# Second attention: two 64-row halves of the array instead of the whole array

## The reference

```python
q, k, v = split(x @ Wqkv + bqkv)          # q: 256 wide, k and v: 64 wide each
q = q.reshape(b, s, 16, 16)               # 16 heads of 16
k = tile(k.reshape(b, s, 4, 16), 4)       # 4 key heads, head h uses key head h % 4
v = tile(v.reshape(b, s, 4, 16), 4)
prob = softmax(q k^T / 16)                # not causal: all 1024 keys
x = layernorm(x + (prob v) @ Wout + bout)
```

## Time and profile before

| | us |
|---|---|
| device time, median of 3 runs | 2425.41 |
| lowest and highest | 2424.32, 2425.58 |
| profiled execution, first to last instruction (its span) | 2423.6 |
| PE busy | 2238.1 (92%) |
| DVE busy | 1561.5 (64%) |
| ACT busy | 1196.9 (49%) |
| DVE's reduction of 512 columns (L1068), mean of 512 | 0.683 |

### The profile page before, as it was taken

The page is one execution under the profiler, slowest core; times in us unless marked ns, Lnnn a source line. Parts: engine busy times, 40 slices in busy tenths (PEclk is TensorE's granted clock), DMA queues, the critical chain, the costliest instruction groups (busy, mean ns, idle before and its releaser), DMA issues. The chain is left out here.

```text
span 2423.6 us, 36462 instructions
## 1 busy us (share of the span) xinstructions
PE 2238.1 (92%) x11264; PEld 1719.0 (71%) x11264; DVE 1561.5 (64%) x2879; ACT 1196.9 (49%) x2397; POOL 567.5 (23%) x550
## 2 busy tenths in 40 slices
PE   6999999999999999679999669999998689999996
PEld 5888888888888888558788434554543458877885
DVE  4666666666666666646566558887882436655665
ACT  4555555555555555344334316666666334433442
POOL 2333333333333333112222210000000012222221
PEclk9999999999999999879999869999999769999998
DMA  2000000000000000011111061212210011111111
GB/s 66 16 17 16 15 16 16 16 15 15 15 15 15 15 9 1 1 38 46 46 46 46 9 145 24 30 27 37 31 26 12 1 38 46 48 50 39 46 49 47
DMA packets 45297, 73.19 MB, mean 30 GB/s; under 512 B 6651, under 2 KB 21798, under 8 KB 44710
## 3 DMA queue, kind: packets, MB, share of 16 engines
q1 hardware_dynamic: 44710, 72.10, 12.2%
q10 hardware_dynamic: 512, 0.13, 0.0%
HBM read 64.74 MB, written 7.34 MB: 30 GB/s over the span
## 5 line engine op out<-in xcount | busy, mean ns | idle before, releaser
L1399 POOL TENSOR_TENSOR a_pr<-a_pr,a_rinv 128x128 f32<-128x128 f32 (+7 forms) x256 | 294.0, 1149 | 598.0 <-DVE a_rinv L1636 598.0
L1068 DVE TENSOR_REDUCE a1m_part<-psum 128x1 f32<-128x512 f32 x512 | 320.8, 683 | 93.4 <-PE psum L914 92.8
L1040 ACT ACTIVATE a1m_pt<-psum 128x512 f32<-128x512 f32 x512 | 265.6, 604 | 115.7 <-PE psum L934 107.6
L647 DVE SCALAR_TENSOR_TENSOR f_hid<-psum,f_bias_now,f_act_s 128x512 f32<-128x512 f32 x168 | 126.0, 750 | 267.0 <-ACT f_act_s L604 196.9
L504 POOL TENSOR_TENSOR f_lo_gu<-f_raw_gu,f_hi_gu 128x512 fp32r<-128x512 f32 x84 | 109.1, 1298 | 783.2 <-ACT f_hi_gu L579 783.2
L604 ACT ACTIVATE f_act_s<-psum,f_bias_now 128x512 f32<-128x512 f32 x168 | 115.7, 689 | 337.4 <-PE psum L71 263.8
L1563 ACT ACTIVATE a_pth<-psum 128x512 fp32r<-128x512 f32 (+3 forms) x384 | 174.6, 490 | 193.6 <-PE psum L1455 192.6
L69 PE MATMUL psum<-xh,f_hi_gu 128*128 128x512 f32 x672 | 265.9, 396 | 2.0 <-POOL f_lo_gu L504 1.3
L71 PE MATMUL psum<-xh,f_lo_gu 128*128 128x512 f32 x672 | 264.3, 393 | 0.0
L70 PE MATMUL psum<-xl,f_hi_gu 128*128 128x512 f32 x672 | 263.6, 392 | 0.0
L914 PE MATMUL psum<-a_ks,a_qm 128*128 128x512 f32 x512 | 224.2, 452 | 23.6 <-DMA a_qm<-a_qd 20.9
(11 more groups left out here) (225 smaller groups left out, 4937.4 us busy)
## 6 DMA issues: line engine op xcount, KB each, us to landing
f_raw_gu<-in_gu SPq DMA_DIRECT2D x84, 256.0 KB, 2.7
a_wr<-in_qkv SPq DMA_DIRECT2D x32, 384.0 KB, 3.1
f_raw_dn<-in_down SPq DMA_DIRECT2D x84, 128.0 KB, 2.0
a_qm<-a_qd SPq DMA_DIRECT2D x48, 128.0 KB, 5.3
a_qt<-a_qd SPq DMA_DIRECT2D x48, 128.0 KB, 3.9
yT<-in_xT SPq DMA_DIRECT2D x4, 512.0 KB, 6.1
a_wor<-in_o SPq DMA_DIRECT2D x16, 128.0 KB, 2.0
a_qd<-a1p_hi SPq DMA_DIRECT2D x2, 1024.0 KB, 14.0
```

The source lines that it names most:

```text
L1040: act.activation(pt[:, kp % 2, g, k, :], st_ps[:, bank(place(c, kp, g, k)), :], ACT.Exp, scale=1.0 / HD1).then_inc(exp_done, 1)
L1068: dve.tensor_reduce(part[:, c, q, g, half:half + 1], mx_ps[:, bank(at + g * 2 + half), :], AX.X, ALU.max).then_inc(mx_taken, 1)
L1399: pool.tensor_tensor(pr[:, j, 0:n], pr[:, j, 0:n], rinv[:, j:j + 1].to_broadcast([P, n]), ALU.mult).then_inc(p_done, 1)
```

## The change

Only `grouped_attention` is changed. Keys and queries lie twice in the height of the array: key heads 0 and 1 on rows 0 to 47, heads 2 and 3 on rows 64 to 111 (`HALFP`), two heads side by side in each half. The row of ones and of maxima is row 48 of each half, and every matmul of maxima or scores takes 48 or 49 rows of one half. The order pairs them: in a step `i` the maxima are those of a head of one half and the two scores those of the heads of the other half. One q tile (`qq`, three places) replaces `qm` and `qt`. Maxima go to a ring of two places of two banks each: both halves of the keys, one reduction over 1024 columns straight into `negm`. The turns of `zt` and `negm` take one place of that ring, at step 9 of a unit. `values` is called once for each key pair (16 records). SP, not ACT, sends the maxima. The loops are written out. The new main part (`...` marks what is left out):

```diff
     ROWS = 3 * HD1
-    MROW = 64
+    HALFP = 64
...
-    NS = NK * G1
-    NM = NQ * G1 * 2
-    NR = 3
-    ORDER = ("s0t1", "s0tv1")
+    QSLOT = 3
     W = KV1 // G1 * 2
     with Phase(nc, tag, psum) as ph:
         qd = [nc.dram_tensor(f"{tag}_qd{s}", (D + KV1, T), F32, kind="Internal").ap() for s in range(2)]
-        ks = ph.sb("ks", [P, B, G1, S], F32R)
+        ks = ph.sb("ks", [P, B, 2, S], F32R)
         vs = ph.sb("vs", [P, NTOK, G1, W])
-        qm = ph.sb("qm", [P, NCH, G1, CH], F32R)
-        qt = ph.sb("qt", [P, NCH, G1, CH], F32R)
+        qq = ph.sb("qq", [P, QSLOT, 2, CH], F32R)
...
-                    for r, src in enumerate((qd[0], qd[1], qd[0])):
-                        sp.dma_start(ks[r * HD1:(r + 1) * HD1, b, :, :].bitcast(F32),
-                                     src[D:D + KV1, b * S:(b + 1) * S].rearrange("(g p) t -> p g t", p=HD1)).then_inc(k_in, 16)
+                    for r in range(2):
+                        for x, src in enumerate((qd[0], qd[1], qd[0])):
+                            p0, d0 = r * HALFP + x * HD1, D + r * 2 * HD1
+                            sp.dma_start(ks[p0:p0 + HD1, b, :, :].bitcast(F32),
+                                         src[d0:d0 + 2 * HD1, b * S:(b + 1) * S].rearrange("(s p) t -> p s t", p=HD1)).then_inc(k_in, 16)
...
-                pool.memset(ks[:].bitcast(F32), 0.0).then_inc(cleared, 1)
-                pool.wait_ge(cleared, 1)
-                pool.memset(ks[MROW:MROW + 1, :, :, :].bitcast(F32), 1.0).then_inc(cleared, 1)
+                pool.memset(ks[:].bitcast(F32), 1.0).then_inc(cleared, 1)
+                pool.memset(vs[:], 0.0).then_inc(cleared, 1)
                 pool.wait_ge(cleared, 2)
-                pool.memset(vs[:], 0.0).then_inc(cleared, 1)
+                pool.memset(vs[:, :, :, HD1:HD1 + 1], 1.0).then_inc(cleared, 1)
                 pool.wait_ge(cleared, 3)
-                pool.memset(vs[:, :, :, HD1:HD1 + 1], 1.0).then_inc(cleared, 1)
-                for t in (qm, qt):
-                    pool.memset(t[:].bitcast(F32), 0.0).then_inc(cleared, 1)
-                pool.wait_ge(cleared, 6)
...
-            st_ps = am.ps([P, NR, CH])
-            mx_ps = am.ps([P, NR, CH])
+            mx_ps = am.ps([P, 2, 2, CH])
+            st_ps = am.ps([P, 3, CH])
...
-            misc_ps = am.ps([P, CH])
...
+            UNITS = [(b, j, c) for b in range(B) for j in range(QUADS) for c in range(NCH)]
+            LAST = len(UNITS) - 1
+            STEPS = NK * G1 // 2
+            GROUPS = (0, 2, 1, 3)
+            TURN = 9
+            def head_of(i):
+                return i // G1, GROUPS[i % G1]
+            def maxima_at(u, i):
+                v, n = (u + 1, STEPS // 2 + i) if i < STEPS // 2 else (u + 2, i - STEPS // 2)
+                return (v, n) if v <= LAST else None
+            FIRST = [(0, i) for i in range(STEPS)] + [(1, i) for i in range(STEPS // 2)]
+            class Ring:
+                def __init__(self):
+                    self.n, self.maxima, self.turns = 0, 0, 0
+                    self.freed = []
+                def place(self):
+                    self.n += 1
+                    return (self.n - 1) % 2, self.freed[self.n - 3] if self.n > 2 else None
+                def a_max(self):
+                    at = self.place()
+                    self.maxima += 1
+                    self.freed.append(((mx_taken, self.maxima),))
+                    return at
+                def a_turn(self, u, with_z, with_m):
+                    at = self.place()
+                    self.freed.append((((z_done, u),) if with_z else ()) + (((m_kept, u + 2),) if with_m else ()))
+                    return at
...
+                def fetch(u):
+                    b, j, c = UNITS[u]
+                    if u >= QSLOT:
+                        sp.wait_ge(st_ready, (u - QSLOT + 1) * 2 * STEPS)
+                    for r in range(2):
+                        for x, src in enumerate((qd[0], qd[0], qd[1])):
+                            d0 = (j * G1 + r * 2) * HD1
+                            rows = src[d0:d0 + 2 * HD1, b * S + c * CH:b * S + (c + 1) * CH]
+                            p0 = r * HALFP + x * HD1
+                            sp.dma_start(qq[p0:p0 + HD1, u % QSLOT, :, :].bitcast(F32),
+                                         rows.rearrange("(s p) t -> p s t", p=HD1)).then_inc(q_in[u % QSLOT], 16)
+                def send_maxima(u):
+                    sp.wait_ge(m_kept, u + 1)
+                    for g in range(G1):
+                        p0 = (g // 2) * HALFP + ROWS
+                        sp.dma_start(qq[p0:p0 + 1, u % QSLOT, g % 2, :].bitcast(F32),
+                                     mrow[g * NQ:(g + 1) * NQ, u % 2, :].bitcast(F32)).then_inc(m_in[u % QSLOT], 16)
+                for u in range(QSLOT):
+                    fetch(u)
+                for u in range(LAST + 1):
+                    send_maxima(u)
+                    if u >= 1 and u + QSLOT - 1 <= LAST:
+                        fetch(u + QSLOT - 1)
...
+                def room(at):
+                    for sem, n in at[1] or ():
+                        pe.wait_ge(sem, n)
+                    return at[0]
+                def maxima(u, i, half, bank):
+                    b, j, c = UNITS[u]
+                    q, g = head_of(i)
+                    p0 = (g // 2) * HALFP
+                    if i == 0 and half == 0:
+                        pe.wait_ge(q_in[u % QSLOT], (u // QSLOT + 1) * 96)
+                    m = pe.matmul(mx_ps[:, bank, half, :], qq[p0:p0 + ROWS, u % QSLOT, g % 2, q * P:(q + 1) * P],
+                                  ks[p0:p0 + ROWS, b, g % 2, half * CH:(half + 1) * CH], start=True, stop=True)
+                    if half == 1:
+                        m.then_inc(mx_ready, 1)
+                def scores(u, i, k):
+                    b, j, c = UNITS[u]
+                    n = u * 2 * STEPS + 2 * i + k
+                    kt, g = i // 2, (1 - i % 2) * 2 + k
+                    p0 = (g // 2) * HALFP
+                    if i == 0 and k == 0:
+                        pe.wait_ge(m_in[u % QSLOT], (u // QSLOT + 1) * 64)
+                    if n >= 3:
+                        pe.wait_ge(exp_done, n - 2)
+                    pe.matmul(st_ps[:, n % 3, :], ks[p0:p0 + ROWS + 1, b, g % 2, kt * P:(kt + 1) * P],
+                              qq[p0:p0 + ROWS + 1, u % QSLOT, g % 2, :], start=True, stop=True).then_inc(st_ready, 1)
+                def values(u, kp):
+                    b, j, c = UNITS[u]
+                    pe.wait_ge(exp_done, (u * NP + kp + 1) * 2 * G1)
+                    if kp == 0 and u >= 1:
+                        pe.wait_ge(zt_done, u)
+                    for k in range(2):
+                        kt = kp * 2 + k
+                        for g in range(G1):
+                            m = pe.matmul(acc_ps[g * W:(g + 1) * W, :], vs[:, b * NK + kt, g, :], pt[:, kp % 2, k, g, :],
+                                          start=kt == 0, stop=kt == NK - 1, tile_position=(0, g * W))
+                    m.then_inc(pv_done, 1)
+                def turn(u, with_z, with_m, bank):
+                    if with_z:
+                        pe.wait_ge(zt_done, u)
+                        for q in range(NQ):
+                            m = pe.transpose(mx_ps[:, bank, 0, q * P:(q + 1) * P], zt[:, q * P:(q + 1) * P], ident[:])
+                        m.then_inc(z_turned, 1)
+                    if with_m:
+                        pe.wait_ge(mx_taken, (u + 2) * STEPS)
+                        pe.transpose(mx_ps[0:G1 * NQ, bank, 1, 0:P], negm[:, (u + 1) % 2, :], ident[:]).then_inc(m_turned, 1)
+                for u, i in FIRST:
+                    bank = room(ring.a_max())
+                    for half in range(2):
+                        maxima(u, i, half, bank)
+                    if (u, i) == (0, STEPS - 1):
+                        turn(-1, False, True, room(ring.a_turn(-1, False, True)))
+                for u in range(LAST + 1):
+                    for i in range(STEPS):
+                        ahead = maxima_at(u, i)
+                        if ahead:
+                            bank = room(ring.a_max())
+                            if ahead:
+                                maxima(*ahead, k, bank)
+                            scores(u, i, k)
+                        if i % 4 == 1 and (u, i) != (0, 1):
+                            values(*((u, i // 4 - 1) if i > 1 else (u - 1, NP - 1)))
+                        if i == TURN and (u > 0 or u < LAST):
+                            turn(u, u > 0, u < LAST, room(ring.a_turn(u, u > 0, u < LAST)))
+                values(LAST, NP - 1)
+                turn(LAST + 1, True, False, room(ring.a_turn(LAST + 1, True, False)))
...
+                def keep_maxima(u):
                     act.wait_ge(m_turned, u + 1)
+                    if u >= 2:
+                        act.wait_ge(m_in[(u - 2) % QSLOT], ((u - 2) // QSLOT + 1) * 64)
```

(102 more changed lines are left out.)

172 lines of the change are left out of this document (21 added, 151 removed).

## The result

The changed kernel takes 2463.31 us (median of 4 runs, 2456.22 to 2467.13) against 2425.49 (4 runs, 2424.32 to 2427.80). The ratio is 1.0152, with a 95% interval of [1.0133, 1.0172]: 1.5% slower, clear of noise. The forecast was 2402.5, with a range of 2386 to 2446.

The account below looks back on a forecast made before the run. PE, busy 92%, was taken to set the pace. Start -2.0, fourteen units -24.3, end +1.9, fetch and keys +1.5 gave -22.9: span 2400.7, plus 1.8, 2402.5 us; range 2386 to 2446.

Parts of the forecast that it names:

- The pairs: Maxima and scores on PE: two matmuls in different halves run side by side, 0.23 us a pair, 7.4 instead of 14.7 a unit.
- The maxima: DVE reductions over 1024 columns: 1.22 us alone, 1.14 each back to back, against 2 x 0.60 before.
- What is late next, the walk: Following PE's queue and the two-place ring: DVE hole of 1.14 us at four values calls, unit 24.1 us.
- Case A: Rival: halves don't overlap; hole 1.83 us, unit 26.9, 40 us more than the forecast, 2443; chance 0.15.
- The clock: PE's granted clock in the main part: forecast signs had it at 1.00; its fall was left to a rival.
- The sum: Adding the second attention's stages: fourteen units 336.4 against 360.7; all changes together -22.9 us.
- case C: Rival: PE's new pauses lower its clock; 34 us a unit at 1.2 GHz, a fifth of the time so 2431; chance 0.09.
- Short height alone costs and gives nothing: Maxima and scores: matmuls over 9 rows follow each other at 0.23 us, as those over 128 do.
- The end: Second attention's main part after the fourteen units: 34.0 us against 32.1 now, so +1.9.
- The start: First maxima until the mrow copy of unit 1: 46.9 us against 48.85 now, so -2.0.
- fetch and keys: Start of second attention: first maxima wait for six transfers (1.0 us), keys need 12 issues (0.5); +1.5 together.
- ACT's transfers to SP: Unit ends: SP issues the four maxima transfers, removing 1.4 us of a unit.

Follow-up runs that it names:

- e5: Changed kernel with 63 and 64 rows per half instead of 48 and 49, zeros in the rows between: 2437.71 us.
- e10: Changed kernel with all key heads from row 0 and 127 and 128 rows, so no halves overlap: 2446.10 us.
- e1: Kernel before, with maxima and scores over 48 and 49 rows instead of 128, order and rings as before: 2701.92 us.
- e3: Changed kernel plus two useless 49-row matmuls before the wait for the ring in two of four steps: 2443.45 us.
- e9: Kernel before, with only the maxima transfers issued by SP instead of ACT: 2415.95 us.
- e4: Changed kernel with values in two calls of eight records instead of one of sixteen: 2391.20 us.
- e7: Kernel before, with maxima and scores over 65 rows instead of 128, still a whole-array tile: 2509.81 us.
- e2: Changed kernel with all heads from row 0, tiles still 48 and 49 rows, so halves cannot overlap: 2572.58 us.
- e6: Changed kernel with values in two calls (e4) and 63 and 64 rows per half (e5) together: 2383.09 us.

## Why the prediction was wrong

**The pairs: right.** In the lines shown they start 0.00 to 0.01 us apart. The Trainium skill ("TensorE: Matmul & The Clock Gate", Part 3) says that row groups run concurrently, and the trace of after now agrees.

**The maxima: right.** Alone a reduction takes 1.22 us, four in a row 4.62 (forecast 4 x 1.14 + 0.08 = 4.64).

**What is late next, the walk: right at full clock.** Hole 1.08 (1.14), period 5.70 (5.70), values 1.92 (1.85), unit 24.4 in e5 (24.1). Case A, walked the same way, came out 3 us off in e10. The walk even gave the price of the low level: values 3.6 us, 34 us a unit. At 3.50 instead of 1.08 a unit of the changed kernel would be 24.4 + 4 x 2.4 = 34.1.

**The clock: wrong, and this is the step that failed.** The sum takes every unit at 1.00, and case C, which has it fall, got 0.09. Two sentences led there. "Short height alone costs and gives nothing" came from two matmuls over 9 rows, 0.23 apart. These rows show what a short matmul takes at a clock granted already, not what clock is granted to a stream of them; e1 puts 276 us to that. And "the new order is more like the last unit", where the clock held at 1.00 through pauses, compared the pauses alone, and not closely: the last unit's matmuls were 128 rows high, and PE was busy 16.50 of 18 us there, 92%, where the new order leaves it 85%. In their place the runs show a mean clock of 0.86 in the units, which rises to 0.94 with 15 rows more (e5) and to 0.93 with the pauses partly filled (e3).

**How much it was.** The excess of a unit over its time at full clock is 27.6 - 24.4 = 3.2 us, times 14, 45 us; with 9.7 us a unit for all of it at the low level, that is a third of the time, and the granted 0.86 says (1 - 0.86) / 0.5 = 28%. The units are 50.1 us over their forecast of 336.4; the other 5 are the size of the unit at full clock. The end is 9.4 us over its forecast, at 0.70. The start is 5.5 over (52.36 against 46.9); its second stretch ran at 0.59, where the kernel before soon had 0.96. What lies before the first maxima was forecast 1.5 longer and came 1.9 shorter, so that no run shows a cost of fetch and keys: -3.4. What follows is 2.9 longer. Together that is the 64.6 us between the two spans. Case C named the right effect and, by e3, a part of the cause; the height it did not have. It put a fifth of the time at the low level, 2431; a third of the units, the end and the start make 2463.

**ACT's transfers to SP**: sized at 1.4 us a unit, measured 0.8 alone in e9; there PE is busy 348.48 of 349.69 us, so that no more was to be had.

**Halves or order?** With tall tiles and no halves the change costs 19.6 us (e10, against 2426.49 for before beside it), by the holes and the short ring; halves at 64 rows give back 8.4 of it (e5), less than the 40 of the walk. At full clock the halves are worth 37 us on fourteen units (378.66 in e10, 1478.38 to 1857.04, against 14 x 24.4); e5's units give 20 of that back at their mean clock of 0.94 (362.29), and its end 8 (41.47 us against 33.36 in e10). What was left in the changed kernel was a path on which DVE waited for values; with these split (e4) the pairing pays.

**Left open.** What in the height counts. R has two pairs of runs for it in which the kind of tile stays: 128 and 65 rows over the whole array (before and e7, 84 us) and 48 and 63 rows in halves (the changed kernel and e5, 26 us). But 64 rows in one half gave 2685 and 65 over the whole array 2510, which R alone doesn't explain, and nothing separates one row from the wider tile. No run has tall tiles with all the pauses of the overlapping kernel, so whether pauses alone would lower the clock isn't shown. What makes the level rise in the middle of an unchanged stream (e1, e7) isn't either. And e2, with pauses and 48 rows, had a clock of 0.75 where e1 had 0.50 without a pause: neither theory explains that.

## What to carry to other kernels

Before packing short matmuls into halves, ask what clock the stream will be granted. Duration rows of short matmuls don't answer. One run of the old kernel with the short tiles gives warning (e1), though not the size: 276 us there, 38 in the changed kernel. Where the idle rows can be zeros, filling them cost nothing here (units of 319.38 us in e4 and e6). And when matmuls get cheap, look at the longest call that stands in PE's queue between two releases of the ring: splitting it brought 72 us (e4 against the changed kernel). About 23 of these are the unit at full clock (24.4 to 22.8 us), most of the rest the clock that no longer falls.

## What the runs showed of the hardware that was not expected

- The same stream of instructions, with only the rows passed over changed: granted clock 1.00 with 128 rows; 0.53 and then 1.00 with 65; 0.50 for 500 us with 64 and with 49, with PE busy all the time, and later 1.00 for 50 us and more.
- In the changed kernel and its kin: 48 rows in two halves 0.86, with useless matmuls in the pauses 0.93, with the values split 1.00; 64 rows in two halves 0.94; 128 rows without halves 1.00.
- e5's ten runs spread over 16 us, e6's four over 3: the one had a mean clock of 0.94 in its units, the other 1.00.
